# A three-stage conv kernel on one core: a ring of 21 tiles in place of 20, image 1's first eight chunks counted during image 0's first group, and one left-neighbour term in four moved from VectorE to TensorE

## What is computed

```python
# layer 0: shift each channel by a fraction of a pixel (4 neighbours), then a 1x1 conv
x = x + einsum('bchw,oc->bohw', bilinear_shift(_gn(x), theta_s) * w_dw, w_pw)
# layer 1
ll, lh, hl, hh = haar_dwt(_gn(x))                      # 128 x 128 pixels from here on
h = gelu(batchnorm(conv1x1(concatenate([ll, lh, hl, hh]), w_c1, b_c1)))
res = h
o = dwconv3x3(h, dw_w, dw_b)                           # depthwise, 9 taps
o = conv1x1(gelu(conv1x1(layernorm_chw(o), pw1_w)), pw2_w)
h = gelu(batchnorm(conv1x1(o + res, w_c2, b_c2)))      # 512 channels
x = x + haar_idwt(h)
```

## Time and profile before

| | before |
|---|---|
| median of 3 runs (lowest to highest) | 5349.4 us (5344.71 to 5351.09) |
| profiled execution: time, span | 5349.64 us, 5348.0 us |
| busy: PE, DVE, ACT, POOL | 4636.7, 4607.9, 4341.1, 1152.0 us |
| granted PE clock, mean | 0.962 |

### The profile page before, as it was taken

How to read it: one execution, slowest core, us unless ns; L and a number is a source line. 1 busy time by engine, 2 the same in 40 slices (tenths; PEclk the granted TensorE clock), 3 DMA queues, 4 the chain that set the end, 5 groups by cost and what they waited for, 6 DMA issues and landing times. The chain is left out here.

```text
span 5348.0 us, 54815 instructions
## 1 busy us (share of the span) xinstructions
PE 4636.7 (87%) x12574; PEld 2144.3 (40%) x12574; DVE 4607.9 (86%) x4207; ACT 4341.1 (81%) x6467; POOL 1152.0 (22%) x855
## 2 busy tenths in 40 slices
PE   2789999999999999999998999999987777777775
PEld 1233334344343443444443666666642222222222
DVE  7999899898998989999907999999568888888887
ACT  5788888888888888888846888888578888888887
POOL 0000000000000000000005888888301111111111
PEclk7999999999999999999999999999999999999998
DMA  8999999999999999998972333333159999999999
GB/s 337 346 351 362 426 404 414 425 383 425 394 414 425 381 425 400 416 405 332 381 283 95 134 134 135 136 136 135 51 113 225 236 236 236 236 235 236 235 236 224
DMA packets 248866, 1542.05 MB, mean 288 GB/s; under 512 B 29424, under 2 KB 29808, under 8 KB 91504
## 3 DMA queue, kind: packets, MB, share of 16 engines
q1 hardware_dynamic: 156528, 936.14, 44.9%
q0 software_dynamic: 36864, 268.45, 24.2%
q10 hardware_dynamic: 55296, 335.57, 15.0%
HBM read 877.35 MB, written 662.70 MB: 288 GB/s over the span
## 5 line engine op out<-in xcount | busy, mean ns | idle before, releaser
L1142 PE MATMUL ps<-arena,c2T 128*128 128x512 f32 x2048 | 1024.3, 651 | 366.8 <-ACT arena L891 364.5
L963 PE MATMUL ps<-arena 128*128 128x512 f32 x2048 | 980.8, 623 | 40.2 <-DMA arena<-out_x 23.3
L941 PE MATMUL ps<-arena 128*128 128x512 f32 x2048 | 966.0, 598 | 45.1 <-DVE arena L1365 22.4
L936 PE MATMUL ps<-arena 128*128 128x512 f32 x1536 | 740.7, 605 | 79.7 <-DVE arena L1349 35.2
L1142 PEld LDWEIGHTS ps<-arena,c2T 128*128 128x128 f32 x2048 | 401.4, 205 | 989.0 <-ACT arena L891 559.7
L891 ACT ACTIVATE arena<-ps,small 128x512 f32<-128x512 f32 x1024 | 713.7, 778 | 98.6 <-DVE arena L1574 90.1
L1333 DVE SCALAR_TENSOR_TENSOR arena<-arena,shift 128x2048 f32<-128x2048 f32 x256 | 601.8, 2351 | 162.0 <-DMA arena<-in_x 100.9
L1458 DVE SCALAR_TENSOR_TENSOR ps<-arena,taps,ps 128x256 f32<-128x256 f32 (+1 forms) x604 | 655.8, 1133 | 19.6 <-PE ps L1087 19.0
L605 ACT ACTIVATE ps<-arena 128x1024 f32<-128x1024 f32 x512 | 526.4, 1028 | 159.8 <-ACT arena L642 146.9
L521 POOL TENSOR_SCALAR arena<-arena 128x256 f32<-128x256 f32 x112 | 103.9, 936 | 2518.8 <-DMA arena<-in_x 2387.3
L642 ACT ACTIVATE arena<-ps,small 128x1024 f32<-128x1024 f32 x512 | 565.0, 1104 | 91.1 <-PE ps L941 89.3
(11 more groups left out here) (169 smaller groups left out, 5907.7 us busy)
## 6 DMA issues: line engine op xcount, KB each, us to landing
arena<-in_x SPq DMA_DIRECT2D x508, 1024.0 KB, 14.4
out_x<-arena ACTq DMA_DIRECT2D x256, 1024.0 KB, 9.0
out_x<-arena POOLq DMA_DIRECT2D x256, 1024.0 KB, 17.0
arena<-out_x SPq DMA_DIRECT2D x208, 1024.0 KB, 16.7
y_dram<-arena ACTq DMA_DIRECT2D x128, 512.0 KB, 8.5
arena<-y_dram SPq DMA_DIRECT2D x128, 512.0 KB, 3.6
h_dram<-arena SPq DMA_DIRECT2D x112, 512.0 KB, 2.7
arena<-h_dram SPq DMA_DIRECT2D x112, 512.0 KB, 10.2
```

The costliest lines, as they stand in the source:

```text
L936: mm(ps[:, r, :], w_right[:, :], u_buf[k][:, 2 * r:2 * r + 2, 2:W + 2], start=False, stop=False, skip_group_check=True)
L941: last = mm(ps[:, r, :], w_center[:, :], v_buf[k][:, r * BANK:(r + 1) * BANK], start=False, stop=True, skip_group_check=True)
L963: last = mm(ps[:, 4 + s % 2, :], w_c1b[:, q, :], cells[:, q // 2, q % 2, :, :], start=(q == 0), stop=(q == 3))
L1142: last = mm(ps[:, 4 * k + q, :], c2T[:, q, :], h2[:, k * HC:(k + 1) * HC], start=True, stop=True)
```

## The change

Three edits go together; memory freed by one is used by another.

**Ring.** RING is 21 (OLD_LAG 20), HEAD is 19. To fit, the buffers `o_squares` and `pool_b` go: `square_o(t)` now writes its squares, which nobody reads, over `pool_sum[t % 2]`, and `make_product(t)` writes straight into `pool_sum[t % 2]`, where POOL adds to it in place. So `square_o` must come after the finish of its tile and before the product of tile t+2, and it moves: ACT runs `square_o(s - 2)` as the last operation of each step, for all tiles. `w_pw1b` and `bias_pw1` get two buffers, since with the longer lag an image's last tile is still to be multiplied when the next scale is made.

**Counting.** Image 1's chunks 0 to 3 are loaded into `x1_buf` and 4 to 7 into `ahead`, right behind image 0's loads. In image 0's first group each of the four steps counts two of them, on DVE and ACT alike; the four counts that followed the group are gone.

**Left neighbour.** For chunk 1 of each group of image 0, DVE leaves L1359 out. PE adds two matmuls of `w_left` for each half (four per chunk), and takes u in place of v for the centre.

```diff
-HEAD = 18
+HEAD = 19
-RING = 20
+RING = 21
 OLD_LAG = RING - 1
...
+        def first_pairs(s):
+            return [divmod(n, SLOTS) for n in (2 * s, 2 * s + 1)]
+        def left_on_pe(b, s):
+            return isinstance(b, int) and b == 0 and s == 1
...
-            for s in range(SLOTS):
-                load_x_ahead(1, 0, s)
+            sp.wait_ge(setup_done, 1)
+            for s in range(SLOTS):
+                sp.dma_start(x1_buf[s], x[1, :, s * CH:(s + 1) * CH]).then_inc(second_in[s], 16)
+            for s in range(SLOTS):
+                wait_alone(sp, nth(NCH - SLOTS + s), x_counted, x_summed)
+                sp.dma_start(ahead[s], x[1, :, (SLOTS + s) * CH:(SLOTS + s + 1) * CH]).then_inc(ahead_in[s], 16)
...
             def make_product(t):
-                if t:
-                    act.wait_ge(pool_step, pool_done(t - 2) + 2)
-                nc.scalar.activation(rows(pool_b), h_tile(t, *POOL_TAPS[1]), ACT.Copy,
+                if t >= 2:
+                    act.wait_ge(o_squared, nth(t - 2))
+                nc.scalar.activation(rows(pool_sum[t % 2]), h_tile(t, *POOL_TAPS[1]), ACT.Copy,
...
-                if 0 <= s - 3 < TILES and (s - 3) % NT != NT - 1:
-                    square_o(s - 3)
                 if q >= 1:
                     copy_hT(q - 1, 0)
...
-                if 0 <= s - 2 < TILES and (s - 2) % NT == NT - 1:
+                if 0 <= s - 2 < TILES:
                     square_o(s - 2)
...
+                    for r in range(2 * half, 2 * half + 2) if left_on_pe(b, s) else ():
+                        mm(ps[:, r, :], w_left, u_buf[k][:, 2 * r:2 * r + 2, 0:W],
+                           start=False, stop=False, skip_group_check=True)
...
-                if ahead_of and not late:
+                if pairs:
+                    count_x(1, *pairs[0])
+                elif ahead_of and not late:
                     count_x(*ahead_of, s, range(0, 2))
...
-                if first_image:
-                    for s in range(SLOTS):
-                        count_x(1, 1, s)
```

More of the change, by code:

```diff
@@ L144, in preact_kernel @@
         hT_buf = [cut(4 * (P + 1)).rearrange("p (k c) -> p k c", k=4) for _ in range(2)]
-        o_squares = cut(TILE // 2).bitcast(BF16)
-        pool_a, pool_b = (cut(TILE) for _ in range(2))
-        w_pw1b = cut(P)
+        pool_a = cut(TILE)
+        w_pw1b = [cut(P) for _ in range(2)]
         pool_sum = [cut(TILE) for _ in range(2)]
@@ L272, in preact_kernel @@
         first_in = [sem(f"first_in{s}") for s in range(SLOTS)]
+        second_in = [sem(f"second_in{s}") for s in range(SLOTS)]
         x1_loaded = [sem(f"x1_loaded{s}") for s in range(SLOTS)]
@@ L635, in take_x1 @@
                         act.wait_ge(c1_done, nth(b * NCH + s, NCH))
+                    if place == "second" and isinstance(b, int) and b == 0:
+                        act.wait_ge(x_counted, nth(NCH + s))
+                        act.wait_ge(x_summed, nth(NCH + s))
                     if place == "held" and s >= 2 * SLOTS - HELD and not (isinstance(b, int) and b == 0):
@@ L663, in sum_x @@
                 q = b * NCH + g * SLOTS + s
-                chunk, arrived, count = first_chunk(g, s) if isinstance(b, int) and b == 0 else \
-                    (ahead[s], ahead_in[s], ahead_count(b, g))
+                chunk, arrived, count = counted_chunk(b, g, s)
                 act.wait_ge(arrived, count)
@@ L732, in shift_group @@
                             act.wait_ge(mom_ready, b * 2 + 2)
-                        sum_x(*ahead_of, s)
+                        if first and isinstance(b, int) and b == 0:
+                            for pair in first_pairs(s):
+                                sum_x(1, *pair)
+                        else:
+                            sum_x(*ahead_of, s)
                     if chunk:
@@ L813, in make_a @@
                 nc.scalar.activation(a_buf, z_bank(q).rearrange("p a n -> p (a n)"), ACT.Gelu,
[L814 removed]
+                                     bias=bias_pw1[q // NT % 2]).then_inc(a_ready, 1)
             def copy_hT(q, half):
@@ L1335, in shift_rows @@
                 late = last and s == 0
+                pairs = first_pairs(s) if first and isinstance(b, int) and b == 0 else None
                 if first and s == 1:
@@ L1380, in image @@
             def image(b, before, tail, following, beyond):
-                first_image = isinstance(b, int) and b == 0
                 for s in range(SLOTS):
-                    shift_rows(b, 0, s, before, tail, (b + 1, 0 if first_image else 1) if following else None, "first")
-                if first_image:
-                    for s in range(SLOTS):
-                        count_x(1, 1, s)
+                    shift_rows(b, 0, s, before, tail, (b + 1, 1) if following else None, "first")
                 with dve.Fori(1, NG - 1) as g:
```

89 lines of the change are left out of this document (51 added, 38 removed).

## The result

The changed kernel takes 5362.6 us (median of 11 runs, 5356.6 to 5368.2), the kernel before, run beside it, 5347.3: the ratio is 1.0027, with a 95% interval of 1.0019 to 1.0035. It is 15 us slower; 5364.5 was forecast. The profiled execution has a span of 5363.1 us, 15.1 more than before.

What follows compares the result with a forecast made beforehand. No single engine was taken to bound the kernel: DVE in image 0 with ACT near, PE in the middle stage's head. Image 0's -9.1, then +14, +2 and +8.0 us on 5349.64 gave 5364.5 us; range 5342 to 5380.

Steps and rivals of the forecast that it cites:

- Counting: Image 0, group 0: DVE's standstill for loads goes; group 1 starts at 139.3 in place of 153.7, 14.4 us gained.
- Left neighbour: Image 0: ACT waits 2.4 us for PE's long half; groups 2-6 lose 0.95 each, group 1 2.2; last saves 1.6.
- Squares behind the tap, in the head: Middle stage's head: two tiles take 12.3 us where PE's 10.3 bound before; seven pairs, +14 us.
- Full steps and norms: Middle stage: full steps absorb the later squares; 0.3 us for each of seven norm steps, +2 us (0 to 5).
- Ring and HEAD: Middle stage: the lag of 20 lengthens the start and gives the drain one tile more; +8.0 us (5 to 12).
- The start: Middle stage, around norm step 18: one step more, with PE coming back at half clock; +1.6 us.
- the drain: End of the middle stage: one tile more outside the overlap, +6.4 us.
- The first: Rival: DVE's saving comes through in all groups of image 0, giving 5343.5 us; chance 0.12.
- The rule of the most occupied engine: Skill's advice to optimise the busiest engine first: relieving DVE in image 0 would shrink a group from 34.2 to 31.95.
- The third rival: Norm steps: the longer ring removes PE's waits of 8.6 and 7.8 us, giving 5348; chance 0.10.
- The fourth: Rival: PE's clock falls to 1.2 GHz in a third of the head, +24 us, 5388; chance 0.07.
- The fifth: Rival: loads for group 0 or 1 of image 0 come late, up to +14 us, 5378; chance 0.07.

Runs made afterwards that it cites:

- experiment 1: The kernel before with only the counting edit (left neighbour on DVE, ring 20, HEAD 18, old squares order): 5332.5 us, ratio 0.9968.
- experiment 2: The changed kernel with image 0's left neighbour back on DVE in all four chunks of a group: 5359.1 us, ratio 1.0017.
- experiment 5: The kernel before with only the squares' order changed (product and squares share a buffer; ring 20, HEAD 18): 5369.3 us, ratio 1.0034.
- experiment 4: The changed kernel with the head's first 15 tiles in ACT's old order and a separate product buffer: 5350.9 us, ratio 1.0003.
- experiment 6: The changed kernel with ACT's two sums over an ahead chunk cut from 512 to 64 columns in image 0: 5355.5 us, ratio 1.0012.
- experiment 9: The counting edit with two weight and bias sets, plus PE adding the left neighbour for two of eight rows in every image 0 chunk: 5317.4 us.
- experiment 7: The kernel with only the counting edit, given two sets of weights and bias: 5330.3 us, ratio 0.9963.
- experiment 10: The counting edit with two weight and bias sets, plus four 256-column PE matmuls before the wait for c1's weights: 5324.0 us, ratio 0.9952.

## Why the prediction came out right, step by step

- **Counting**, -14.4: of this 12.1 is the counting, and the edit alone brings 12.7 in image 0's trace, 17 us in the runs. The other 2.3 is the operation that DVE leaves out in chunk 1 of group 0. DVE did get through group 0 by 139.04 (139.3 forecast), but began group 1 at 140.67: the ring's load for it landed only at 140.46. The prediction put the ring's loads at nothing, on the ground that the same operations wait for them as before. With DVE earlier than before they came late, by 1.63 us here and 1.28 in group 1; experiment 1, in which DVE comes to group 1 at 141.2, has neither wait.
- **Left neighbour**: the mechanism was right, the size was not. With the 2.3 us of group 0 taken in, its terms come to +5.3 - 2.3 = +3.0; it is +6.1 in image 0 (experiment 2) and 5 in the runs. In group 0 it saved 0.6 and not 2.3, by the late load. The wait of 2.4 us was there to the hundredth (2.36), but group 1 did not lose the 2.2 us: it was 0.5 shorter, DVE's 2.25 of saved work less waits of 1.28 for the load and 0.32 for PE. Groups 2 to 6 lost 0.7, 1.2, 1.7, 1.6 and 1.7, and not 0.95 each; from group 3 on this is because ACT's chunk takes 8.39 us there and not 8.2. The last group kept 0.2 of its saving, not 1.6.
- **Squares behind the tap, in the head**, +14: +14.1, in experiment 5 with nothing else, and taken back in full by experiment 4. Pairs of 12.3 us were forecast; they are 5.15 + 7.14 = 12.29. This is the term that carries the result, and it is right in mechanism and size.
- **Full steps and norms**, +2: too small. The squares alone cost 4.2 between the first and the last norm (3 to 6, by the spread of the other kernels). The kernels with the late squares take 129.6 to 129.8 from the first to the second norm, those with the old order 126.1 to 128.5.
- **Ring and HEAD**, +8.0: last norm to last h2 is +7.4, in all four kernels with the ring of 21 (the changed one and experiments 2, 4 and 6) and in none with 20. The start was priced at +1.6, and the drain at +6.4. The start lies between the first and the second norm, and that stretch is 129.7 in the changed kernel and 129.8 in experiment 5 with its ring of 20. So nothing is seen of it, and the drain has the whole. Between all norms the kernels with the ring of 21 are 0.4 to 1.4 above experiment 5, which is within the spread.
- **Not in the sum**: images 1 to 7, -5.3. Without it the span would have grown by 20, not by 15. That the forecast of +14.9 was hit within 0.2 us is luck: this offset what was too small in image 0 (2.4), between the norms with the start (1.9) and in the drain (1.0). Some 3.1 of it is the clock (last section), in images 1 and 5, and 2.1 is group 3 of image 1, whose cause is open. None of it can be pinned on the change: over the ten kernels without filling these images take 2263.5 to 2271.0 us in one execution each, the changed kernel being the lowest.
- **Rivals.** The first (DVE's saving comes through) is refuted for this edit by experiments 2 and 6. Yet it holds for another way to make the same saving, experiment 9. The rule of the most occupied engine would have been right about what to relieve and wrong about this way of doing it. The third rival's waits, 8.6 and 7.8 us before, did not go with the second set (8.7 and 7.8 in experiment 7) nor with the ring of 21 (8.8 and 7.8 in the changed kernel). The fourth, a low clock in the head, did not come: the granted clock is 1.00 from 2828 to 2920 us. The fifth, late loads, came in part: the 2.9 us of waits in image 0 told above, of the 14 that it gave as the most.

## What to carry to other kernels

Where two engines hand halves of a buffer to each other, look at the longest half and not at the sum: eight matmul records in one chunk of four cost 6 us, and the same eight spread evenly gained 12. Ask, when an engine gets to a place earlier, whether the loads that it wants there are issued earlier too. Follow the loop of the engine that is "only" 84% busy before taking work off the one at 100%. In a pipelined loop, put last what waits for a neighbour's newest result only if nothing that this neighbour wants stands behind it.

## What the runs showed of the hardware

**A low clock behind a stop of TensorE.** In images 1 to 6 of every kernel without filling, the second group takes either 39.4 to 39.6 us or 40.9 to 41.2, and it is the shorter where the granted clock over its beginning is 1.00. Granted clock over its first 6 us, images 2 to 5, before and in experiment 10 (columns: window, length, PE busy (records), PEclk, DMA share, GB/s):

```profile
773.00:779.00 6.00, 5.38 (x12) 1.00 1.01 408
1106.00:1112.00 6.00, 5.62 (x9) 0.72 1.02 423
1440.00:1446.00 6.00, 5.72 (x9) 0.72 1.01 411
1775.00:1781.00 6.00, 5.91 (x10) 0.72 1.00 397
```

```profile
760.00:766.00 6.00, 6.00 (x17) 1.00 1.01 399
1092.00:1098.00 6.00, 5.42 (x13) 1.00 1.01 419
1424.00:1430.00 6.00, 6.00 (x14) 1.00 0.99 401
1756.00:1762.00 6.00, 5.93 (x14) 1.00 1.01 413
```

The stop ahead of these matmuls, before in images 2 and 3, and in experiment 10 in image 3:

```profile
773.62 2.96 PE L963 MATMUL ps<-arena 128*128 128x512 f32 x6 [1.61 <-DVE small L1308]
...
1106.38 3.37 PE L963 MATMUL ps<-arena 128*128 128x512 f32 x4 [2.33 <-DVE small L1308]
```

```profile
1090.10 1.89 PE L1001 MATMUL ps<-arena,ident 128*128 128x256 f32 x8
1092.58 3.84 PE L994 MATMUL ps<-arena 128*128 128x512 f32 x8 [0.60 <-DVE small L1344]
```

Four records in 3.37 us against six in 2.96: part of them ran at 1.2 GHz. In images 1 to 6 of all these traces a stop of at most 1.7 us never brought the clock down, and one of 2.3 to 3.4 us mostly did, but not in four cases (2.37, 2.46, 2.84 and 3.2 us). In image 7 a stop of 1.88 us had it in experiment 5 (0.76 over the first 7 us), and one of 2.54 had not in experiments 2 and 9. So the length of that one stop is not the whole of it. Each fall costs 1.6 us, and which images it hits differs between traces of kernels that are alike in these images: a part of the difference between two kernels that no edit explains.

**Loops with addresses from a register.** ACT's chunk takes 172.52 - 164.34 = 8.18 us in the groups that are written out, and 272.47 - 264.08 = 8.39 in groups 3 to 5, which are a loop over groups (rows of experiment 9): the wait from a take to the put behind it is 0.41 in the one and 0.63 in the other. It is a bound only once ACT is. That the register's address is the cause was not tested.
